# A causal mask moved from a TensorE product to a VectorE add in PSUM

## The reference

```
# layer 1: conditioned attention, 16 heads of 32, no mask
xn = rms_norm(x, g_norm) * (1 + scale) + shift        # scale, shift from cond @ W_emb + b_emb
q, k, v = split(xn @ W_qkv);  q, k = rms_norm(q), rms_norm(k)
o = softmax(q k^T / sqrt(32)) v;   x1 = o + o @ W_out
# layer 2: latent causal attention, 16 heads of 32, then a mixture of experts
h = x1 + attention(rmsnorm(x1, ln1), ..., causal=True)
out = h + shared_expert(n) + sum over the 2 best of 7 routed experts of weight * expert(n),  n = rmsnorm(h, ln2)
result = x + out
```

## Time and profile before

| | us |
|---|---|
| median of 3 runs (lowest, highest) | 1292.27 (1285.44, 1299.75) |
| the profiled execution: its time, its span | 1290.86, 1289.1 |
| PE busy, DVE busy, ACT busy in it | 1169.7, 744.4, 572.3 |
| phase 2 steps: from 574.5 to 963 | 388.5 |

### The profile page before, as it was taken

How to read it: one execution, slowest core, us unless ns; L and a number is a source line. 1 busy time by engine, 2 the same in 40 slices (tenths; PEclk the granted TensorE clock), 3 DMA queues, 4 the chain that set the end, 5 groups by cost and what they waited for, 6 DMA issues and landing times.

```text
span 1289.1 us, 18670 instructions
## 1 busy us (share of the span) xinstructions
PE 1169.7 (91%) x6059; PEld 825.7 (64%) x6059; DVE 744.4 (58%) x1807; ACT 572.3 (44%) x1248; POOL 290.7 (23%) x244
## 2 busy tenths in 40 slices
PE   5979999999999889999999989989999999999970
PEld 5745555665566446557767757766657888888850
DVE  6565675477545856666565575566364774444433
ACT  3324464345443555455465454455264753222210
POOL 1313122100210031001011200200124464555530
PEclk9979999999999999999999999999899999999995
DMA  7064243125311732352284264265357744555559
GB/s 255 33 180 131 65 136 112 50 86 184 99 50 58 225 107 57 99 189 88 88 259 149 86 234 122 84 201 176 86 186 232 262 152 105 109 108 113 115 134 331
DMA packets 88127, 178.42 MB, mean 138 GB/s; under 512 B 12609, under 2 KB 23265, under 8 KB 86497
## 3 DMA queue, kind: packets, MB, share of 16 engines
q1 hardware_dynamic: 79216, 156.90, 37.4%
q0 software_dynamic: 8512, 19.93, 8.2%
q10 hardware_dynamic: 304, 0.40, 0.2%
HBM read 110.86 MB, written 65.27 MB: 137 GB/s over the span
## 4 chain that ended last, share of the span: by engine, by line
PE 77%; DVE 8%; DMA 5%; ACT 4%; issue 3%; SPq 1%; POOL 0%; DVEq 0%; ACTq 0%; POOLq 0%
PE psum L862 14%; PE psum L681 9%; PE psum L682 8%; PE psum L683 8%; PE psum L846 6%; PE psum L825 6%; PE psum L690 4%; PE psum L940 4%; PE psum L942 4%; PE psum L941 4%; PE psum L967 2%; PE psum L969 2%; PE psum L968 2%; PE psum L909 2%; PE psum L772 2%
## 5 line engine op out<-in xcount | busy, mean ns | idle before, releaser
L1174 ACT ACTIVATE probs<-psum 128x512 f32<-128x512 f32 (+3 forms) x512 | 257.3, 517 | 231.5 <-PE psum L849 120.6
L825 PE MATMUL psum<-stack 96*128 96x512 f32 (+3 forms) x512 | 210.2, 416 | 8.6 <-DMA stack<-split_s 4.0
L1583 DVE TENSOR_REDUCE nmax<-psum 128x1 f32<-128x512 f32 x256 | 170.5, 684 | 77.0 <-PE psum L825 73.2
L846 PE MATMUL psum<-stack 97*128 97x512 f32 (+3 forms) x512 | 197.3, 386 | 16.8 <-ACT probs L1174 15.4
L862 PE MATMUL psum<-probs,vals 128*33 128x512 f32 (+3 forms) x1024 | 209.4, 531 | 0.0
L1586 DVE CUSTOM_DVE_ANT_0 psum<-psum,causal 128x128 f32<-128x128 f32 (+3 forms) x256 | 123.0, 501 | 21.0 <-PE psum L825 19.4
L825 PEld LDWEIGHTS psum<-stack 96*128 96x128 f32 x512 | 100.0, 196 | 46.3 <-issue 23.7
L846 PEld LDWEIGHTS psum<-stack 97*128 97x128 f32 x512 | 99.0, 193 | 40.0 <-ACT probs L1174 25.8
L862 PEld LDWEIGHTS psum<-probs,vals 128*33 128x33 f32 x1024 | 49.8, 112 | 99.6 <-issue 65.5
L681 PE MATMUL psum<-w_hi,xh 128*128 128x512 f32 (+1 forms) x256 | 95.4, 373 | 4.2 <-DVEq L1449 2.5
L682 PE MATMUL psum<-w_hi,xl 128*128 128x512 f32 (+1 forms) x256 | 93.6, 366 | 0.0
(11 more groups left out here) (238 smaller groups left out, 2338.0 us busy)
## 6 DMA issues: line engine op xcount, KB each, us to landing
stack<-split_s SPq DMA_DIRECT2D x378, 128.0 KB, 3.0
split_s<-split SPq DMA_DIRECT2D x64, 512.0 KB, 3.0
xt<-in_x_dram SPq DMA_DIRECT2D x4, 1024.0 KB, 5.2
x_s<-yt SPq DMA_DIRECT2D x4, 1024.0 KB, 5.0
xt<-x_s SPq DMA_DIRECT2D x4, 1024.0 KB, 4.8
yt<-in_x_dram SPq DMA_DIRECT2D x4, 1024.0 KB, 5.6
res<-x_s SPq DMA_DIRECT2D x4, 1024.0 KB, 8.2
acc_s<-yt SPq DMA_DIRECT2D x4, 1024.0 KB, 6.0
```

The source lines that it names most:

```text
L825: sq.filled(nc.tensor.matmul(psum[:, sq.bank(M), 0:n], st[:, 0, t * P:(t + 1) * P], st[:, 1, 0:n], start=True, stop=True), M)
L846: last = nc.tensor.matmul(psum[:, bank, lo:S], st[:, 1, t * P:(t + 1) * P], st[:, 0, lo:S], start=True, stop=not masked)
L1174: sk.cleared(nc.scalar.activation(probs[:, M % NX, lo:S], psum[:, sk.bank(M), lo:S], ACT.Exp, scale=SCALE), M)
L1583: sq.cleared(V.tensor_reduce(out, psum[:, sq.bank(M), :], AX.X, ALU.max, negate=True), M)
```

## The change

The product L849 goes away, and with it `identr`, the two copies on ScalarE and the waits for `r_ok`. `mask` is fp32 and written by GpSimd directly. In phase 2 VectorE has a new instruction at each step, `hide(M)`: it waits for `scores_t(M)`, adds `mask` to the diagonal block in PSUM in place, and counts the new semaphore `hidden_`, for which the exponential of step M now waits in place of the product. VectorE's order at a step of phase 2 was `maximum(M+16)`, pieces of `M`; it is `maximum(M+16)`, `hide(M)`, pieces of `M-1`. Its pieces move one step back and one add stands ahead of them. Nothing changes for the other engines' orders, the DMAs or phase 1.

```diff
@@ scores_t (TensorE)
-                last = nc.tensor.matmul(psum[:, bank, lo:S], st[:, 1, t * P:(t + 1) * P], st[:, 0, lo:S],
-                                        start=True, stop=not masked)
-                if masked:
-                    last = nc.tensor.matmul(psum[:, bank, lo:lo + P], identr[:, :], mask[:, :], start=False, stop=True)
-                sk.filled(last, M)
+                sk.filled(nc.tensor.matmul(psum[:, bank, lo:S], st[:, 1, t * P:(t + 1) * P], st[:, 0, lo:S],
+                                           start=True, stop=True), M)
@@ TensorE, VectorE: ahead of the steps
-            pe.wait_ge(r_ok, 2)
-            dve.wait_ge(r_ok, 2)
@@ ScalarE
-            copy(identr[:, :], ident[:, :]).then_inc(r_ok, 1)
-            copy(mask[:, :], vs[:, 0, 0:P]).then_inc(r_ok, 1)
...
-                sk.wait_full(act, M)
+                if phase(k) == 2:
+                    act.wait_ge(hidden_, M - NSTEPS // 2 + 1)
+                else:
+                    sk.wait_full(act, M)
@@ VectorE
+            def hide(M):
+                t = head_step(M)[2]
+                sk.wait_full(dve, M)
+                x = psum[:, sk.bank(M), t * P:(t + 1) * P]
+                V.tensor_tensor(x, x, mask[:, :], ALU.add).then_inc(hidden_, 1)
...
             for M in range(NSTEPS):
                 if M + LEAD < NSTEPS:
                     maximum(M + LEAD)
-                if M < NSTEPS:
-                    (the pieces of step M)
+                k, m = divmod(M, STEPS_H)
+                if phase(k) == 2:
+                    hide(M)
+                    beside_step(M - 1)
+                if M < NSTEPS // 2 - 1:
+                    beside_step(M)
...
+            beside_step(NSTEPS - 1)
```

More of the change, by code:

```diff
@@ L273, in build @@
         small = Strip(SMALL_AT)
-        ident, identr = small("ident", [P, P]), small("identr", [P, P], F32R)
+        ident = small("ident", [P, P])
         below = small("below", [P, P])
@@ L278, in build @@
         logits = small("logits", [P, B * NT, NE])
-        mask = small("mask", [P, P], F32R)
+        mask = small("mask", [P, P])
         modall = small("modall", [P, B, 2 * NC])
@@ L378, in build @@
         v_ld, v2_ld = sem("vectors_loaded"), sem("small_tables_loaded")
-        c_ok, r_ok, m_ok = sem("constants_ready"), sem("rounded_constants_ready"), sem("vals_and_stack_set")
+        c_ok, m_ok, hidden_ = sem("constants_ready"), sem("vals_and_stack_set"), sem("scoresT_masked")
         ones_ok = sem("ones_set")
@@ L1256, in _ @@
             nc.gpsimd.memset(ident[:, :], 0.0).then_inc(c_ok, 1)
-            nc.gpsimd.memset(vs[:, :, 0:P], 0.0).then_inc(c_ok, 1)
+            nc.gpsimd.memset(mask[:, :], 0.0).then_inc(c_ok, 1)
             nc.gpsimd.memset(causal[:, :], 0.0).then_inc(c_ok, 1)
@@ L1262, in _ @@
                                     pattern=[[-1, P]], channel_multiplier=1).then_inc(c_ok, 1)
-            nc.gpsimd.affine_select(out=vs[:, 0, 0:P], in_=vs[:, 0, 0:P], compare_op=ALU.is_ge, fill=NEG, base=0,
+            nc.gpsimd.affine_select(out=mask[:, :], in_=mask[:, :], compare_op=ALU.is_ge, fill=NEG, base=0,
                                     pattern=[[1, P]], channel_multiplier=-1).then_inc(c_ok, 1)
@@ L1587, in maximum, with beside_step @@
                                                       op0=ALU.add, op1=ALU.min, accum_out=out), M)
+            def hide(M):
[3 more added lines that the diff above has]
+                V.tensor_tensor(x, x, mask[:, :], ALU.add).then_inc(hidden_, 1)
+            def beside_step(M):
+                for key in BESIDE[M // STEPS_H].get(M % STEPS_H, ()):
+                    if key[0] == "w2":
+                        n = key[1]
+                        if n < NC:
+                            dve.wait_ge(w2_ld, 7 * 16)
+                            w = w2_raw[:, n * 512:(n + 1) * 512]
+                            V.tensor_scalar(w, w, vcol[:, 28 + n:29 + n], None, ALU.mult).then_inc(w2_sc, 1)
+                    elif key[0] not in ("wo1", "wo2", "ws"):
+                        beside(key)
             for n in range(2):
@@ L1622, in _ @@
                     maximum(M + LEAD)
-                if M < NSTEPS:
[L1624 to L1636, removed]
+                k, m = divmod(M, STEPS_H)
[4 more added lines that the diff above has]
+                    beside_step(M)
+                if k == LAST and m == 1:
+                    ring.wait_full(dve, ("v", LAST, NT - 1))
+                    V.memset(ones[:, :], 1.0).then_inc(ones_ok, 1)
+            beside_step(NSTEPS - 1)
             def lo_of_x(i):
```

## The result

| | before | after |
|---|---|---|
| median, us | 1293.2 (4 runs, 1285.4 to 1299.8) | 1352.1 (4 runs, 1350.3 to 1357.0) |
| profiled execution: span | 1289.1 | 1348.5 |
| first to last `scores_t` of phase 2 | 574.5 to 962.8 | 574.7 to 1021.2 |

A forecast was written before the change was run, and what follows sets the result against it. TensorE was taken to lead, VectorE and ScalarE following with little to spare in places. A 23 us product saving against waits of 14.8 + 8 + 3.6 + 5.5 gave +8.9 on 1290.9: 1300 us, own range 1283 to 1305 (0.55).

The forecast's parts named there:

- the sum: Over the 32 groups of phase 2: -23 + 14.8 + 8 + 3.6 + 5.5 = +8.9 us.
- The walk: Last batch, steps 10 to 17, followed by rows: +1.4 us for the group instead of a pure saving of -0.72.
- bare group: Eight steps of phase 2 with no products beside them to cover the longer way; 7 such, 2.1 us each, +14.8.
- at nothing: Terms priced zero; for VectorE's moved pieces, bank releases late by under 1 us, which PE covers with the next step's products.
- The product's cost: Mask product on TensorE in phase 2: 0.09 us each (0.06 to 0.11), 256 of them 23 us (15 to 28).
- The waits together: Phase 2 losses: bare groups +14.8, five with one bare half +8, two with DVE nearly full +3.6, 18 others +5.5 us.
- The walk through a bare group: Last batch's second half, from the start of scores(30): scores_t(16) at 1.78, 0.66 later; scores_t(17) at 3.18, 1.14 later.
- The full groups: Groups of phase 2 with products beside the steps: PE has time; a full one keeps 0.5 to 0.7 us.
- The slack of 1.55 us: First batch, exponential 15 to scores_t(17): exponential comes 1.4 us later, so the slack just holds and the saving stays.
- The add's load: 256 adds at 0.21 us put 54 us more on DVE in phase 2, 231 to 285 of 388; fits on average.
- the dense and the remaining groups: Two groups with DVE nearly full, 1.8 us each, +3.6; 18 others, some 11 losing 0.5 each, +5.5.
- The slower one: VectorE's queue becomes the bound in full groups too; 18 groups lose 1.3 us each, +23; 1306 to 1322; chance 0.35.

The follow-up runs named there:

- e11_noprod: The kernel before with only the mask product (L849) deleted and the keys-side mask left out; 1282.4 us, ratio 0.993.
- e2_none: The changed kernel without the add and its wait, keys-side mask left out, VectorE's pieces still one step later; 1299.8 us, ratio 1.008 to before.
- e3_aside: The changed kernel, mask left out, with a 128x128 SBUF add for which only VectorE waits; 1319.5 us, ratio 1.023 to before.
- e4_tiny: The changed kernel with the add covering 4 columns instead of 128, adding zeros, exponential still waiting for it; 1337.4 us, ratio 1.036 to before.

## Why the prediction was wrong

- *The first step that failed: the sum prices TensorE at the full clock throughout.* The walk itself said that PE would stand still twice in each bare group; what this does to the granted clock was left out. The clock was at half for 88.7 us of phase 2 in place of 17.1, which is worth some 24 to 31 us by the rate of phase 1 and at most 32. The last batch went from 81 to 103 us in place of 86.
- *The second: "at nothing" for the moved pieces.* I named what would be late, the release of the ring's two banks, and priced it at under 1 us, covered by PE. It cost 16 us: the copy out of the bank now waits for a maximum whose scores TensorE issues later.
- *The product's cost* was taken as 0.09 us, 23 us in sum. Its removal alone gave 9 us. In groups that are full of products each gave 0.07 (groups of steps 24 to 31 are 0.53 to 0.57 us shorter in e11_noprod); in the rest part of it vanished in waits. Mis-sized, within a factor of 2.6.
- *The waits together* were about right. From e2_none to the changed kernel the add and its wait cost 52 us. Less the clock's 24 to 31, that leaves 21 to 28, for which the sum had 14.8 + 8 + 3.6 + 5.5 = 32, with part of the unsaved product in it. Two terms left out and one too large, not the walk, make up the distance from +9 to +59.
- *The walk through a bare group* was right, as long as the clock held. Its second half, in the changed kernel at the full clock:

```profile
927.77 0.48 PE L825 MATMUL psum<-stack 96*128 96x512 f32 x1
...
929.69 0.47 PE L846 MATMUL psum<-stack 97*128 97x512 f32 x1 [0.92 <-ACT probs L1171]
...
931.02 0.78 PE L846 MATMUL psum<-stack 97*128 97x512 f32 x1 [0.35 <-ACT probs L1171]
```

  From the start of the scores to `scores_t` two steps on 1.92 us (walk: 1.78), to the next 3.25 (walk: 3.18). VectorE's rows there show the order maximum, add, reciprocal, multiply, maximum, add that the walk assumed:

```profile
928.29 0.70 DVE L1583 CUSTOM_DVE_ANT_0 psum<-psum,causal 128x512 f32<-128x512 f32 x1 [3.74 <-PE psum L825]
...
928.91 0.33 DVE L1590 TENSOR_TENSOR psum<-psum,mask 128x128 f32<-128x128 f32 x1
929.15 0.19 DVE L1520 RECIPROCAL rden<-psum 128x8 f32<-128x8 f32 x1
...
929.72 0.69 DVE L1583 CUSTOM_DVE_ANT_0 psum<-psum,causal 128x512 f32<-128x512 f32 x1
...
930.33 0.33 DVE L1590 TENSOR_TENSOR psum<-psum,mask 128x128 f32<-128x128 f32 x1
```

  A bare group at the full clock went up by 1.3 us, as the row at 648.80 shows; the walk gave 1.4.
- *The full groups didn't keep their saving.* The slack of 1.55 us was read rightly but under wrong names: the rows at 610.85 and 612.67 are the exponential of step 23 and `scores_t(25)`, not steps 15 and 17. "The group keeps its saving" then failed: steps 16 to 23 of the three full batches are 0.57 us shorter without the product (e11_noprod), but in the changed kernel only 0.01, 0.01 and 0.23. The 15 groups without half clock lose 9.1 us; that this equals the forecast for all 32 is chance, since the terms of the sum give about -2 for these 15.
- *The add's load.* By averages VectorE had room for 54 us. As load alone the adds cost 20, with 24 us more at the half clock; the terms of the dense and the remaining groups together were 9.
- *The rivals.* The slower one (1306 to 1322, VectorE's queue binds in full groups too) named the right direction and the right mechanism for the waits (e3_aside, e4_tiny, the full groups). Less the clock's estimated share, 1321 to 1328 us would be left, at its upper end or just above. The clock is in no rival.

What stays open is the clock's exact share in phase 2: 24 to 31 us is carried over from stretches without the add, and no run took the clock's fall away there while leaving the waits.

## What to carry to other kernels

A product that is issued right behind another on a busy TensorE can cost far less than its busy time (here 0.07 us of 0.24). Moving it to an engine whose result lies between TensorE and a ring of two banks puts that engine's whole queue into the loop. Walk the loop by rows first, and then ask what the idle time it makes does to TensorE's clock: here each us at the half clock cost 0.34 to 0.44 us, about half of what the forecast missed. Pieces that free a bank are not free to move either, even by one step.

## What the hardware showed unexpectedly

- TensorE's granted clock was at half for 88.7 us of phase 2 in place of 17.1, while TensorE was idle ahead of `scores_t` for exponentials for 31 us. The eight `pv` products of four steps took 3.20 us in place of 1.70.
- The same 62 products of a group in phase 1 took 15.11 us at the full clock and 18.09 with 6.8 us of them at the half clock; the clock's fall there differs from run to run.
- A kernel with some 40 us more of products ran in nearly the same time (1356.7 against 1352.1).
- A 128-wide fp32 add in place in PSUM takes 0.33 us, and the next VectorE instruction starts 0.24 behind it; a maximum of the same width takes 0.29 and 0.21.
- The mask product in bf16 in place of fp32r made no measurable difference (ratio 0.999, 0.997 to 1.002).
